# Latent attention: both score halves in a row, then all six transposes, copied in one go

## The chip, the cores and the metric

The kernel runs on one core of a Trainium2 chip. The metric is the device time of one execution in microseconds (us). TensorE does the matmuls and writes to PSUM, which has eight banks of 512 fp32 columns a partition; ScalarE and VectorE read PSUM, GpSimd doesn't; SyncE issues the DMAs.

## The reference

The program is a chain of four blocks over 2,048 tokens of width 128: a state space block, a local transformer of two layers, a latent attention, and a mixture of experts, with a normalisation behind each. The change touches the latent attention alone. Cut to its core, with 16 heads of width 64 and latents of width 64:

```
c_q, c_kv = h @ w_down_q.T, h @ w_down_kv.T
q = rope((c_q @ w_up_q.T) by head)
k = rope((c_kv @ w_up_k.T) by head)
v = (c_kv @ w_up_v.T) by head
attn = softmax(q k.T / 8)
out = (attn v) @ w_out.T + residual
```

Every head attends to all 2,048 keys. All of it is in float32.

## The kernel before, in words

`latent_attention` works through units: a unit is one head and 512 queries (64 units in all), and a step `G` is 128 queries of a unit against the 2,048 keys, so a unit has four steps `r` = 0 to 3. Two heads form a pair with common projections; the loop goes over pairs of heads (four bodies with two pairs each), quarters of the queries `j`, the two heads `w`, and `r`. Eight steps (`w` = 0 and 1, `step` = 4w + r) make one pass; there are 32 passes.

For each step, in two halves of 1,024 keys: TensorE computes the scores into two PSUM banks (`score_pair`, line 1553), VectorE takes the row maximum (`row_max`, 1584), ScalarE the exponential with its sum (`exps`, 1598) into `probs`. Of each half the first three 128-column tiles are transposed by TensorE (`turn_tiles`, 1574) into the bank `turned` and copied by ScalarE to `near` (`copy_tiles`, 1578); the other five are transposed in 32x32 blocks by VectorE (`turn_blocks`, 1684), written to memory by a DMA (1690) and read back reordered into `far` (1695). The values (`mix`, 1614) are multiplied with `near` and `far` one unit later, in eight pairs of matmuls spread over the steps: near pairs at r = 3, far pairs two at r = 0, two at r = 1, one at r = 2 (`MIXED_AT`). `take_mixed` (1622) copies the sum, `output` (1628) multiplies it by the head's output matrix into the two banks `side`, `take_output` (1636) copies these, GpSimd adds them up. Into the same two banks `side` TensorE projects queries and keys of the next pair of heads (`pieces`, 1449); `take_piece` (1569) copies one bank each to `raw`, from which GpSimd makes keys and queries (`make_parts`, 1704, 1455, 1460).

The order of each engine is written out by hand in its block; engines meet at semaphores. The scores of a step are computed one step ahead: in step `G` TensorE issues the scores of `G + 1`, each half as soon as the exponential of that half of `G` has read its banks, and the transposes of `G`. In program order a step of TensorE is: scores of half 0, three transposes, scores of half 1, three transposes, the output products (at step 0 and 6), the values, the pieces (behind the values of step 1 and 3). ScalarE does: what the step has besides (takes, see the listing), copy of half 0, exponential of half 0 of `G + 1`, copy of half 1, exponential of half 1. VectorE does: block transpose of half 1 of `G`, row maxima of both halves of `G + 1`, block transpose of half 0 of `G + 1`. `turned` has one bank, so each group of three transposes waits for the copy of the group before it.

Of the kernel before, what the change touches and what calls it, by code (L numbers as in the profile page):

```python
# [9 lines left out]
ACT = mybir.ActivationFunctionType  # L10
AX = mybir.AxisListType

P = 128
# [3 lines left out]
CH = 512  # L17
# [1285 lines left out]
UNITS = HEADS_G * NC  # L1303
RT = 4
# [3 lines left out]
TURN = NEAR // 2  # L1308
# [5 lines left out]
def latent_attention(nc, dram, const, x, acc):  # L1314

    ident = const["ident"]
# [4 lines left out]
    with Space(nc, "g") as sp:  # L1321
# [4 lines left out]
        with Space(nc, "ga") as s:  # L1326
# [5 lines left out]
            turned = s.ps("turned", [P, 2, CH])  # L1332
# [224 lines left out]
        def pieces(pe, turn, at):  # L1557

            for swap in range(2):
                for kind in range(2):  # L1560
                    ins = projected(side[:, kind, swap * QH:(swap + 1) * QH], turn, kind, swap,
                                    slice(at * QH, (at + 1) * QH))
                    if swap:
                        ins.then_inc(m["piece_full"], 1)

        def take_piece(act, half, kind):
            act.wait_ge(m["parts_ready"], 2 * half + 1 + kind)
            act.wait_ge(m["piece_full"], 2 * half + 1 + kind)
            nc.scalar.activation(raw[:, kind], side[:, kind], ACT.Copy).then_inc(m["piece_taken"], 1)  # L1569

        def turn_tiles(pe, r, half):
            for k in range(TURN):
                at = half * 2 * CH + k * P
                ins = nc.tensor.transpose(turned[:, k * P:(k + 1) * P], probs[:, r % 2, at:at + P], ident[:])  # L1574
            ins.then_inc(m["turn_done"], 1)

        def copy_tiles(act, w, r, half):
            nc.scalar.activation(near[:, w, TURN * half:TURN * (half + 1), r * P:(r + 1) * P],  # L1578
                                 turned[:, 0:TURN * P].rearrange("p (t n) -> p t n", n=P), ACT.Copy).then_inc(m["near_copied"], 1)

# [117 lines left out]
        def make_parts(pool, turn, at, half, kind):  # L1698

            both = raw[:, kind]  # L1700
            first, second = both[:, 0:QH], both[:, QH:]
            n = 8 * half + 3 * kind
            pool.wait_ge(m["piece_taken"], 2 * half + 2 + kind)
            nc.gpsimd.tensor_tensor(both, both, waves[:, at].rearrange("p s n -> p (s n)"), ALU.mult)\  # L1704
                .then_inc(m["order"], 1)
            pool.wait_ge(m["order"], n + 1)
            if kind == 0:
                for head in range(2):
                    place_keys(nc.gpsimd, turn, head, at, QH, first, second).then_inc(m["order"], 1)
                    pool.wait_ge(m["order"], n + 2 + head)  # L1710
            else:
                for crossed in range(2):
                    for head in range(2):
                        place_queries(nc.gpsimd, turn, head, head ^ crossed, at, QH, first, second)\
                            .then_inc(m["order"], 1)
                    pool.wait_ge(m["order"], n + 3 + 2 * crossed)
            pool.sem_inc(m["parts_ready"], 1)
# [3 lines left out]
        with nc.Block() as block:  # L1721

            @block.sync
            def _(sync):
                with sync.Fori(0, PAIRS_G // 2) as i:
                    for turn in range(2):
                        g = 2 * i + turn
                        for j in range(NC):
                            for w in range(2):
# [10 lines left out]
                                if j == 0 and w == 0:  # L1740
                                    sync.wait_ge(m["piece_full"], 2 * H + 2)
                                    load_w(sync, turn, g + 2)
# [41 lines left out]
            def _(pe):  # L1784
# [4 lines left out]
                with pe.Fori(0, PAIRS_G // 2) as i:  # L1789
                    for turn in range(2):  # L1790
                        g = 2 * i + turn
                        for j in range(NC):
                            for w in range(2):
                                U = 8 * g + 2 * j + w
                                for r in range(RT):
                                    G = 4 * U + r
                                    on, head, chunk, at = turn, w, j, r + 1
                                    if r == RT - 1:
                                        head, chunk, at = 1 - w, (j + w) % NC, 0
                                        if w == 1 and j == NC - 1:  # L1800
# [10 lines left out]
                                    if w == 0 and r == 0:  # L1811
                                        pe.wait_ge(m["out_taken"], U + 1)
                                        pe.wait_ge(m["mixed_ready"], U + 1)
                                        pe.wait_ge(mixer_loaded[0], 16 * (4 * g + j + 1))
                                        output(pe, mixer_now[0])
                                    if w == 1 and r == 2:
                                        pe.wait_ge(m["piece_taken"], 2 * (8 * g + 2 * j) + 5)
                                        pe.wait_ge(m["mixed_ready"], U + 1)
                                        pe.wait_ge(mixer_loaded[1], 16 * (4 * g + j + 1))
                                        output(pe, mixer_now[1])  # L1820
                                    if r == 0:
                                        pe.wait_ge(landed[w], 64 * (4 * g + j + 1))
                                    if r == 3:
                                        pe.wait_ge(m["mixed_ready"], U + 2)
                                        pe.wait_ge(m["near_copied"], 8 * U + 1)
                                    mix(pe, w if r < 3 else 1 - w, MIXED_AT[r])
                                    if w == 0 and r == 1:
                                        pe.wait_ge(w_loaded[1 - turn], 16 * (i + 1 + turn))
                                        pe.wait_ge(m["out_taken"], U + 2)
                                        pieces(pe, 1 - turn, 2 * j)  # L1830
                                    if w == 0 and r == 3:
                                        pe.wait_ge(m["piece_taken"], 2 * (8 * g + 2 * j) + 3)
                                        pieces(pe, 1 - turn, 2 * j + 1)
                pe.wait_ge(m["out_taken"], UNITS + 1)
                pe.wait_ge(m["mixed_ready"], UNITS + 1)
                output(pe, mixers[:, HEADS_G + 1])
# [3 lines left out]
                pe.wait_ge(m["near_copied"], 8 * UNITS + 1)  # L1840
                pe.wait_ge(landed[1], 64 * (4 * PAIRS_G + 1))
# [8 lines left out]
            def _(dve):  # L1850
# [30 lines left out]
            def _(act):  # L1881
                act.sem_inc(m["near_copied"], 1)
                act.sem_inc(m["mixed_ready"], 1)
                act.sem_inc(m["piece_taken"], 1)
                act.sem_inc(m["out_taken"], 1)
                for half in range(2):
                    exps(act, 0, 0, half, 0, free=False)
                with act.Fori(0, PAIRS_G // 2) as i:
                    for turn in range(2):
                        g = 2 * i + turn  # L1890
                        for j in range(NC):
                            for w in range(2):
                                U = 8 * g + 2 * j + w
                                H = 8 * g + 2 * j
                                for r in range(RT):
# [5 lines left out]
                                    elif step == 2:  # L1901
                                        take_piece(act, H, 0)
                                        falls(act, H - 1)
                                    elif step == 3:
                                        take_mixed(act, U + 1)
                                        take_piece(act, H, 1)
                                    elif step == 4:
                                        take_piece(act, H + 1, 0)
                                    elif step == 5:
                                        take_piece(act, H + 1, 1)  # L1910
                                    elif step == 6:
# [372 lines left out]
```

## Time and profile before

| | us |
|---|---|
| median of 3 runs (2306.93 to 2310.36) | 2308.57 |
| the profiled execution | 2309.71 |
| its span | 2307.8 |
| TensorE busy (matmuls) | 2063.7 (89%) |
| VectorE busy | 1614.0 (70%) |
| ScalarE busy | 1349.7 (58%) |
| GpSimd busy | 1079.1 (47%) |

The loop of the latent attention runs from about 685 to 2090 us of the span. All times are of one profiled execution. Matmuls are pipelined: a busy TensorE need not be one at its peak, so starts are a better measure than busy times. The clock is that granted to TensorE, as a share of 2.4 GHz.

### The profile page before, as it was taken

To read this page: it belongs to the slowest core of one execution; us is meant where nothing else is said; L and a number is where in the kernel's file an instruction comes from. 1 tells how busy PE (TensorE), PEld (TensorE's weight loads), DVE (VectorE), ACT (ScalarE), POOL (GpSimd) and SP (SyncE) were. 2 spreads that over 40 slices of the span, in tenths; PEclk is the share of its full clock that TensorE was granted. 3 is DMA by queue.
4 is the path that set the end of the run, shared out by engine and by line. 5 is a ranking of instruction groups with operands and counts; after the bars stand their busy time and mean duration, and the time that the engine had idled before them with its cause. 6 is when DMAs were issued, how large, how long until landed. Compare 5 with 4: busy or idle time off the path is not lost. (4 is left out here: it accounts for less than half of the span.)

```text
span 2307.8 us, 37934 instructions
## 1 busy us (share of the span) xinstructions
PE 2063.7 (89%) x11974; PEld 977.9 (42%) x11974; DVE 1614.0 (70%) x2431; ACT 1349.7 (58%) x2907; POOL 1079.1 (47%) x1225
## 2 busy tenths in 40 slices
PE   5848898898669999999999999999999999995597
PEld 2534585476423333333334333333333433432254
DVE  6887665956557777767777776777776777773644
ACT  5425773675117677666776776776766776673111
POOL 0727542833055555545555555555554555553000
PEclk8978899989769999999999999999999999997698
DMA  1001301030145766766766766667666676672000
GB/s 33 1 13 50 72 3 32 1 73 13 52 163 219 255 253 227 261 243 223 259 233 249 260 228 248 225 244 266 227 249 227 238 269 229 245 265 84 35 1 19
DMA packets 195082, 374.26 MB, mean 162 GB/s; under 512 B 11888, under 2 KB 156912, under 8 KB 193840
## 3 DMA queue, kind: packets, MB, share of 16 engines
q1 hardware_dynamic: 194864, 371.61, 45.2%
q8 instruction: 105, 1.72, 0.3%
q14 instruction: 113, 0.93, 0.1%
HBM read 182.82 MB, written 171.44 MB: 154 GB/s over the span
## 5 line engine op out<-in xcount | busy, mean ns | idle before, releaser
L1584 DVE TENSOR_REDUCE g.lowest<-g_score 128x1 f32<-128x1024 f32 x514 | 625.0, 1221 | 217.2 <-PE g_score L1553 214.6
L1598 ACT ACTIVATE g.probs<-g_score,g.lowest 128x1024 f32<-128x1024 f32 x514 | 573.0, 1115 | 117.5 <-DVE g.lowest L1584 117.4
L1553 PE MATMUL g_score<-g.keys,g.queries 64*128 64x512 f32 x2056 | 579.5, 641 | 19.7 <-PEq L1473 10.8
L1684 DVE STREAM_TRANSPOSE g.blocks<-g.probs 128x640 f32<-128x640 f32 x513 | 430.6, 840 | 143.3 <-ACT g.probs L1598 122.8
L1578 ACT ACTIVATE g.near<-g_turned 128x384 f32<-128x384 f32 x512 | 249.7, 488 | 251.0 <-PE g_turned L1574 251.0
L1614 PE MATMUL g_mix_ps<-g.far,mid.y_tok 128*64 128x512 f32 x1320 | 326.0, 607 | 0.0
L1574 PEld LDWEIGHTS g_turned<-top.ident,g.probs 128*128 128x128 f32 x1536 | 159.3, 141 | 391.5 <-issue 198.9
L1574 PE MATMUL g_turned<-top.ident,g.probs 128*128 128x128 f32 x1536 | 281.5, 292 | 0.0
L1553 PEld LDWEIGHTS g_score<-g.keys,g.queries 64*128 64x128 f32 x2056 | 161.9, 186 | 224.5 <-issue 147.9
L1704 POOL TENSOR_TENSOR mid.y_tok<-mid.y_tok,g.waves 128x512 f32<-128x512 f32 x128 | 162.0, 1265 | 192.1 <-ACT mid.y_tok L1569 192.1
L1460 POOL TENSOR_TENSOR g.queries<-mid.y_tok 64x256 f32<-64x256 f32 x256 | 185.2, 724 | 19.6
L1614 PE MATMUL g_mix_ps<-g.near,mid.y_tok 128*64 128x512 f32 x792 | 187.3, 608 | 3.3 <-DMA g.far<-bounce 3.3
L1644 POOL TENSOR_TENSOR g.scaled<-g.scaled,g.coef 128x1024 f32<-128x1024 f32 x67 | 127.1, 1896 | 120.9 <-ACT g.scaled L1636 120.9
L1675 POOL TENSOR_TENSOR g.coef<-g.fall,g.inverse 128x8 f32<-128x8 f32 x65 | 13.2, 202 | 271.9 <-DVE g.inverse L1671 271.9
L1614 PEld LDWEIGHTS g_mix_ps<-g.far,mid.y_tok 128*64 128x64 f32 x1320 | 77.9, 136 | 107.8 <-issue 99.9
L1569 ACT ACTIVATE mid.y_tok<-g_side 128x512 f32<-128x512 f32 x128 | 77.2, 603 | 65.3 <-PE g_side L1449 65.3
L1598 ACT ACTIVATION_READ_ACCUMULATOR g.probs<-g_score,g.lowest 128x1 f32 x514 | 103.1, 201 | 0.0
L1455 POOL TENSOR_TENSOR g.keys<-mid.y_tok 64x256 f32<-64x256 f32 x128 | 92.4, 722 | 10.1
L1614 PEld LDWEIGHTS g_mix_ps<-g.near,mid.y_tok 128*64 128x64 f32 x792 | 51.8, 138 | 93.3 <-issue 93.3
L1650 POOL TENSOR_TENSOR top.x_tok<-top.x_tok,g.scaled 128x512 f32<-128x512 f32 x67 | 85.1, 1270 | 5.3
L1647 POOL TENSOR_TENSOR g.scaled<-g.scaled 128x512 f32<-128x512 f32 x67 | 84.9, 1266 | 5.2
L1636 ACT ACTIVATE g.scaled<-g_side 128x1024 f32<-128x1024 f32 x67 | 69.0, 1030 | 20.6 <-PE g_side L1628 12.6
(364 smaller groups left out, 2893.9 us busy)
## 6 DMA issues: line engine op xcount, KB each, us to landing
g.far<-bounce SPq DMA_DIRECT2D x257, 640.0 KB, 5.8
bounce<-g.blocks SPq DMA_DIRECT2D x256, 640.0 KB, 6.1
g.far<-g.near SPq DMA_DIRECT2D x7, 640.0 KB, 5.7
lt0.v_late<-la0.v SPq DMA_DIRECT2D x6, 512.0 KB, 10.2
lt1.v_late<-la1.v SPq DMA_DIRECT2D x6, 512.0 KB, 10.2
bounce<-g.near SPq DMA_DIRECT2D x4, 640.0 KB, 6.8
top.upto<-g.mixers SPq DMA_DIRECT2D x33, 64.0 KB, 5.6
lt.turns<-turns SPq DMA_DIRECT2D x1, 2048.0 KB, 8.1
```

Of the source, the lines that this page charges most:

```text
L1455: return engine.tensor_tensor(keys[block % 2 * 64:block % 2 * 64 + 64, turn, head, cols], first[head * 64:head * 64 + 64], second[head * 6 ...
L1460: return engine.tensor_tensor(queries[half * 64:half * 64 + 64, turn, head, at * width:(at + 1) * width], first[head * 64:head * 64 + 64], ...
L1553: nc.tensor.matmul(score[:, 2 * pair + odd], queries[rows, turn, head, cols], keys[rows, turn, head, pair * CH:(pair + 1) * CH], start=Tru ...
L1574: ins = nc.tensor.transpose(turned[:, k * P:(k + 1) * P], probs[:, r % 2, at:at + P], ident[:])
L1578: nc.scalar.activation(near[:, w, TURN * half:TURN * (half + 1), r * P:(r + 1) * P], turned[:, 0:TURN * P].rearrange("p (t n) -> p t n", n ...
L1584: nc.vector.tensor_reduce(lowest[:, unit, half, r:r + 1], score[:, 2 * half:2 * half + 2].rearrange("p b n -> p (b n)"), AX.X, ALU.max, ne ...
L1598: nc.scalar.activation(probs[:, r % 2, half * 2 * CH:(half + 1) * 2 * CH], score[:, 2 * half:2 * half + 2].rearrange("p b n -> p (b n)"), ...
L1614: ins = nc.tensor.matmul(out, values[:, at], moving, start=(k == 0), stop=(k == T // 2 - 1))
L1644: nc.gpsimd.tensor_tensor(parts, parts, coef[:, unit].unsqueeze(3).broadcast_to([P, 2, RT, D]), ALU.mult)\
L1650: nc.gpsimd.tensor_tensor(a, a, scaled[:, 0], ALU.add).then_inc(m["added"], 1)
L1684: nc.vector.transpose(blocks[:, r, :, REST * half:REST * (half + 1)].rearrange("p j t c -> p t j c"), probs[:, r % 2, at:at + REST * P].re ...
L1704: nc.gpsimd.tensor_tensor(both, both, waves[:, at].rearrange("p s n -> p (s n)"), ALU.mult)\
```

## The change

Both score halves of a step now stand first, then one wait for the copy of the step before, then all six transposes, into two banks. ScalarE copies the six tiles in one instruction, between its two exponentials. VectorE takes the first row maximum ahead of the block transpose of half 1 of the step before. PSUM has no free bank for this: `turned` and `side` are now three banks with one in common, so in steps 0, 1, 3 and 6 the output products or pieces stand behind the values and wait for the step's own copy, and in steps 1, 2, 4 and 7 the transposes wait until the bank in common has been taken. The pieces of keys and queries are taken by one instruction (steps 2 and 4) in place of two (steps 2 and 3, 4 and 5). The spread of the value pairs over the steps is the same.

```diff
-        turned = sp.ps("turned", [P, CH])
-        side = sp.ps("side", [P, 2, CH])
+        work = sp.ps("work", [P, 3, CH])
+        turned, side = work[:, 0:2], work[:, 1:3]
...
+        def take_pieces(act, half):
+            act.wait_ge(m["parts_ready"], 2 * half + 2)
+            act.wait_ge(m["piece_full"], half + 1)
+            nc.scalar.activation(raw[:], side[:], ACT.Copy).then_inc(m["piece_taken"], 1)
+
+        def turn_tiles(pe, r):
+            for half in range(2):
+                for k in range(TURN):
+                    at = half * 2 * CH + k * P
+                    ins = nc.tensor.transpose(turned[:, half, k * P:(k + 1) * P], probs[:, r % 2, at:at + P], ident[:])
             ins.then_inc(m["turn_done"], 1)
...
+        def copy_tiles(act, w, r):
+            nc.scalar.activation(near[:, w, :, r * P:(r + 1) * P].rearrange("p (k t) n -> p k t n", k=2),
+                                 turned[:, :, 0:TURN * P].rearrange("p k (t n) -> p k t n", n=P), ACT.Copy)\
+                .then_inc(m["near_copied"], 1)
...
-                                    pe.wait_ge(m["exp_done"], 2 * G + 1)
-                                    score_pair(pe, 0, on, head, chunk, at)
-                                    pe.wait_ge(m["near_copied"], 2 * G + 1)
-                                    turn_tiles(pe, r, 0)
-                                    pe.wait_ge(m["exp_done"], 2 * G + 2)
-                                    score_pair(pe, 1, on, head, chunk, at)
-                                    pe.wait_ge(m["near_copied"], 2 * G + 2)
-                                    turn_tiles(pe, r, 1)
...
+                                    for half in range(2):
+                                        pe.wait_ge(m["exp_done"], 2 * G + half + 1)
+                                        score_pair(pe, half, on, head, chunk, at)
+                                    pe.wait_ge(m["near_copied"], G + 1)
+                                    if step == 1:
+                                        pe.wait_ge(m["out_taken"], H + 2)
+                                    elif step == 2:
+                                        pe.wait_ge(m["piece_taken"], H + 1)
+                                    elif step == 4:
+                                        pe.wait_ge(m["piece_taken"], H + 2)
+                                    elif step == 7:
+                                        pe.wait_ge(m["out_taken"], H + 3)
+                                    turn_tiles(pe, r)
...
                                     mix(pe, w if r < 3 else 1 - w, MIXED_AT[r])
+                                    if step in (0, 1, 3, 6):
+                                        pe.wait_ge(m["near_copied"], G + 2)
+                                    if step == 0:
+                                        pe.wait_ge(m["out_taken"], H + 1)
+                                        pe.wait_ge(m["mixed_ready"], U + 1)
+                                        pe.wait_ge(mixer_loaded[0], 16 * (4 * g + j + 1))
+                                        output(pe, mixer_now[0])
...
-                                    turn_blocks(dve, r, 1, G)
                                     if r == 3:
                                         dve.wait_ge(m["combined"], U + 2)
-                                    for half in range(2):
-                                        row_max(dve, unit, (r + 1) % RT, half, G + 1)
+                                    row_max(dve, unit, (r + 1) % RT, 0, G + 1)
+                                    turn_blocks(dve, r, 1, G)
+                                    row_max(dve, unit, (r + 1) % RT, 1, G + 1)
...
-                                    for half in range(2):
-                                        act.wait_ge(m["turn_done"], 2 * G + half + 1)
-                                        copy_tiles(act, w, r, half)
-                                        exps(act, unit, (r + 1) % RT, half, G + 1)
+                                    exps(act, unit, (r + 1) % RT, 0, G + 1)
+                                    act.wait_ge(m["turn_done"], G + 1)
+                                    copy_tiles(act, w, r)
+                                    exps(act, unit, (r + 1) % RT, 1, G + 1)
```

## Rows read from the trace of the kernel before

**Rows 1.** One stretch of the attention stage: length, busy of each engine, granted clock, DMA.

```profile
1100.00:1300.00 200.00, 200.00 (x1030) 78.48 (x1026) 151.57 (x167) 139.65 (x268) 110.92 (x140) 1.00 0.69 250
```

**Rows 2.** What TensorE's matmuls waited for, 700 to 2100 us: total, times, longest.

```profile
PE g_score L1553 <- issue: 8.9, 3, 3.8
PE g_mix_ps L1614 <- DMA g.far<-bounce: 3.3, 1, 3.3
```

**Rows 3.** Timeline of TensorE over one pass: start, duration, instructions.

```profile
1210.51 1.13 PE L1553 MATMUL g_score<-g.keys,g.queries 64*128 64x512 f32 x4
1211.57 0.55 PE L1574 MATMUL g_turned<-top.ident,g.probs 128*128 128x128 f32 x3
1212.04 1.13 PE L1553 MATMUL g_score<-g.keys,g.queries 64*128 64x512 f32 x4
...
1213.58 1.16 PE L1628 MATMUL g_side<-top.upto,g.mixed 64*128 64x128 f32 x16
1214.67 1.94 PE L1614 MATMUL g_mix_ps<-g.far,mid.y_tok 128*64 128x512 f32 x8
1216.54 1.13 PE L1553 MATMUL g_score<-g.keys,g.queries 64*128 64x512 f32 x4
...
1221.48 1.14 PE L1449 MATMUL g_side<-g.c,g.w_up 64*128 64x256 f32 x8
1222.44 1.02 PE L1553 MATMUL g_score<-g.keys,g.queries 64*128 64x512 f32 x4
...
1225.41 1.08 PE L1614 MATMUL g_mix_ps<-g.far,mid.y_tok 128*64 128x512 f32 x4
1226.42 1.13 PE L1553 MATMUL g_score<-g.keys,g.queries 64*128 64x512 f32 x4
...
1251.22 2.79 PE L1614 MATMUL g_mix_ps<-g.near,mid.y_tok 128*64 128x512 f32 x12
1253.95 1.13 PE L1553 MATMUL g_score<-g.keys,g.queries 64*128 64x512 f32 x4
```

**Rows 4.** Timeline of TensorE where the stage begins, and behind the loop's first turn.

```profile
677.53 3.78 PE L1553 MATMUL g_score<-g.keys,g.queries 64*128 64x512 f32 x8 [10.77 <-PEq L1473]
...
1035.21 2.08 PE L1553 MATMUL g_score<-g.keys,g.queries 64*128 64x512 f32 x4 [2.52 <-issue]
```

**Rows 5.** The first of these two as a stretch of TensorE: busy, then granted clock.

```profile
677.50:681.30 3.80, 3.77 (x10) 0.50 0.01 2
```

**Rows 6.** Timeline of the local transformer: eight transposes in a row at full clock.

```profile
423.24 1.09 PE L726 MATMUL lp_turned<-top.ident,lp1.rotated 128*128 128x128 f32 x8
```

**Rows 7.** Timeline of VectorE and ScalarE over the first step of that pass, and later.

```profile
1211.71 1.23 DVE L1584 TENSOR_REDUCE g.lowest<-g_score 128x1 f32<-128x1024 f32 x1 [0.90 <-PE g_score L1553]
...
1213.05 1.11 ACT L1598 ACTIVATE g.probs<-g_score,g.lowest 128x1024 f32<-128x1024 f32 x1 [0.41 <-DVE g.lowest L1584]
...
1213.25 1.23 DVE L1584 TENSOR_REDUCE g.lowest<-g_score 128x1 f32<-128x1024 f32 x1 [0.31 <-PE g_score L1553]
...
1214.15 0.48 ACT L1578 ACTIVATE g.near<-g_turned 128x384 f32<-128x384 f32 x1
1214.39 0.84 DVE L1684 STREAM_TRANSPOSE g.blocks<-g.probs 128x640 f32<-128x640 f32 x1
1214.52 1.12 ACT L1598 ACTIVATE g.probs<-g_score,g.lowest 128x1024 f32<-128x1024 f32 x1
...
1215.61 1.03 ACT L1636 ACTIVATE g.scaled<-g_side 128x1024 f32<-128x1024 f32 x1
1215.76 0.85 DVE L1684 STREAM_TRANSPOSE g.blocks<-g.probs 128x640 f32<-128x640 f32 x1 [0.53 <-ACT g.probs L1598]
...
1223.55 1.23 DVE L1584 TENSOR_REDUCE g.lowest<-g_score 128x1 f32<-128x1024 f32 x1 [0.91 <-PE g_score L1553]
```

**Rows 8.** Timeline behind the loop: a copy, and matmuls that wait for it.

```profile
2110.21 0.59 ACT L1622 ACTIVATE g.mixed<-g_mix_ps 128x512 f32<-128x512 f32 x1
...
2110.85 1.16 PE L1628 MATMUL g_side<-g.mixers,g.mixed 64*128 64x128 f32 x16 [1.61 <-ACT g.mixed L1622]
```

More of the change, by code:

```diff
@@ L1562, in pieces @@
                                     slice(at * QH, (at + 1) * QH))
[L1563 to L1574, printed above, removed]
+            ins.then_inc(m["piece_full"], 1)
+        def take_pieces(act, half):
[7 more added lines that the diff above has]
+                    ins = nc.tensor.transpose(turned[:, half, k * P:(k + 1) * P], probs[:, r % 2, at:at + P], ident[:])
             ins.then_inc(m["turn_done"], 1)
-        def copy_tiles(act, w, r, half):
-            nc.scalar.activation(near[:, w, TURN * half:TURN * (half + 1), r * P:(r + 1) * P],
-                                 turned[:, 0:TURN * P].rearrange("p (t n) -> p t n", n=P), ACT.Copy).then_inc(m["near_copied"], 1)
+        def copy_tiles(act, w, r):
+            nc.scalar.activation(near[:, w, :, r * P:(r + 1) * P].rearrange("p (k t) n -> p k t n", k=2),
+                                 turned[:, :, 0:TURN * P].rearrange("p k (t n) -> p k t n", n=P), ACT.Copy)\
+                .then_inc(m["near_copied"], 1)
         def row_max(dve, unit, r, half, G):
@@ L1702, in make_parts @@
             n = 8 * half + 3 * kind
-            pool.wait_ge(m["piece_taken"], 2 * half + 2 + kind)
+            pool.wait_ge(m["piece_taken"], half + 1)
             nc.gpsimd.tensor_tensor(both, both, waves[:, at].rearrange("p s n -> p (s n)"), ALU.mult)\
@@ L1740, in _ @@
                                 if j == 0 and w == 0:
-                                    sync.wait_ge(m["piece_full"], 2 * H + 2)
+                                    sync.wait_ge(m["piece_full"], H + 1)
                                     load_w(sync, turn, g + 2)
@@ L1809, in _ @@
-                                    pe.wait_ge(m["near_copied"], 2 * G + 2)
-                                    turn_tiles(pe, r, 1)
[L1811 to L1820, printed above, removed]
+                                    step = 4 * w + r
+                                    H = 8 * g + 2 * j
+                                    for half in range(2):
+                                        pe.wait_ge(m["exp_done"], 2 * G + half + 1)
+                                        score_pair(pe, half, on, head, chunk, at)
@@ L1824, in _ @@
                                         pe.wait_ge(m["mixed_ready"], U + 2)
-                                        pe.wait_ge(m["near_copied"], 8 * U + 1)
+                                        pe.wait_ge(m["near_copied"], 4 * U + 1)
                                     mix(pe, w if r < 3 else 1 - w, MIXED_AT[r])
-                                    if w == 0 and r == 1:
+                                    if step in (0, 1, 3, 6):
[5 more added lines that the diff above has]
+                                        output(pe, mixer_now[0])
+                                    elif step == 1:
                                         pe.wait_ge(w_loaded[1 - turn], 16 * (i + 1 + turn))
-                                        pe.wait_ge(m["out_taken"], U + 2)
                                         pieces(pe, 1 - turn, 2 * j)
-                                    if w == 0 and r == 3:
-                                        pe.wait_ge(m["piece_taken"], 2 * (8 * g + 2 * j) + 3)
+                                    elif step == 3:
                                         pieces(pe, 1 - turn, 2 * j + 1)
+                                    elif step == 6:
+                                        pe.wait_ge(m["mixed_ready"], U + 1)
+                                        pe.wait_ge(mixer_loaded[1], 16 * (4 * g + j + 1))
+                                        output(pe, mixer_now[1])
                 pe.wait_ge(m["out_taken"], UNITS + 1)
                 pe.wait_ge(m["mixed_ready"], UNITS + 1)
+                pe.wait_ge(m["near_copied"], 4 * UNITS + 1)
                 output(pe, mixers[:, HEADS_G + 1])
@@ L1839, in _ @@
                 pe.wait_ge(m["mixed_ready"], UNITS + 2)
-                pe.wait_ge(m["near_copied"], 8 * UNITS + 1)
+                pe.wait_ge(m["near_copied"], 4 * UNITS + 1)
                 pe.wait_ge(landed[1], 64 * (4 * PAIRS_G + 1))
@@ L1883, in _ @@
                 act.sem_inc(m["mixed_ready"], 1)
-                act.sem_inc(m["piece_taken"], 1)
                 act.sem_inc(m["out_taken"], 1)
@@ L1901, in _ @@
                                     elif step == 2:
-                                        take_piece(act, H, 0)
+                                        take_pieces(act, H)
                                         falls(act, H - 1)
@@ L1905, in _ @@
                                         take_mixed(act, U + 1)
-                                        take_piece(act, H, 1)
                                     elif step == 4:
-                                        take_piece(act, H + 1, 0)
-                                    elif step == 5:
-                                        take_piece(act, H + 1, 1)
+                                        take_pieces(act, H + 1)
                                     elif step == 6:
```

## The prediction, made before the changed kernel was run

> **What bounds the kernel now.** I read the table of stretches first. In the latent attention stage TensorE is busy for the whole 200 us, at a granted clock of 1.00, beside VectorE 152, ScalarE 140, GpSimd 111 and DMA at 0.69 [rows 1]. The list of TensorE's waits came next: over 1,400 us there are 12 us in which its matmuls stood idle, 8.9 at the loop's turns and one 3.3 us wait for a DMA at the very end [rows 2]. So the stage goes by what TensorE issues, and I lay that out from the timeline. One pass over a pair of units (eight steps) runs from the scores at 1210.51 to the same scores at 1253.95, 43.44 us [rows 3]. A step's scores, transposes, scores, transposes take 3.07 (1210.51 to 1213.58), output products 1.09, two value pairs 1.87, one pair 1.01, three pairs 2.73, the projection pieces 0.96. Scores right behind pieces are 0.1 shorter (busy 1.02 against 1.13). The pass: 8 x 3.07 + 4 x 1.87 + 2 x 1.01 + 2 x 2.73 + 2 x 1.09 + 2 x 0.96 - 2 x 0.1 = 43.42. This agrees with the trace to 0.02, so no wait costs anything in it. There are 32 passes. Every microsecond of TensorE that goes is worth 32, if nothing else is late.
>
> **What TensorE no longer pays.** Scores to transposes take 1.06, transposes to scores 0.47 [rows 3]. Two scores in a row: eight matmul records at a granted clock of 0.50, the 1.2 GHz level, take 3.78; four take 2.08 in the same state (1.13 at full clock), so the second half adds 1.70, which is 0.85 at full clock [rows 3 to 5]. Hence scores, scores, then transposes after 0.85 + 1.06 = 1.91. Three transposes are busy 0.55 [rows 3] and eight in a row 1.09 [rows 6], 0.108 for each further one; six give 0.87, and what follows starts after 0.47 + 3 x 0.108 = 0.80. The front part of a step becomes 2.71 in place of 3.07. The bounds: scores in a row no better than 1.06 apart (nothing gained), six transposes no better than 2 x 0.47 = 0.94. I take 0.85 and 0.80, because both rows show the same instructions in a row. Saved: 0.36 a step, 2.88 a pass, 92 us in all, if nothing is late.
>
> The Trainium skill speaks against the 0.85. "TensorE: Matmul & The Clock Gate", Part 3, The mechanism, says that a weight load passes matmuls in flight only if its row group is another; the second scores load the same two row groups as the first. By it they would be 1.06 apart. The trace at half clock doesn't bear it out; its own result is the fourth case below.
>
> **What is late next.** In the new order a step has this course, counted from its first scores (S0). The first row maximum starts at 1.20 (1210.51 to 1211.71) [rows 3, 7]. The first exponential starts 1.34 behind it, at 2.54, and the next instruction on ScalarE follows 1.10 to 1.11 later [rows 7]. The result of an exponential is there 1.24 after its start (1214.52, the block transpose at 1215.76) [rows 7]: at 3.78. Now the single copy of six tiles stands at 3.65. ScalarE copies 384 elements in 0.48 and 1024 in 1.03 [rows 7]; between them 768 take 0.81, so the copy ends at 4.46, and TensorE goes on 0.05 later (a copy of 0.59 from 2110.21, matmuls at 2110.85) [rows 8]: 4.52. An upper end for it are two old copies, 2 x 0.48 = 0.96; a lower end is 2 x 0.37 = 0.74, the pace at which ScalarE goes from one on to the next instruction (1214.15 to 1214.52). VectorE now does maximum, block transpose of the old second half, maximum. Row maximum to block transpose is 1.14 (1213.25 to 1214.39), and the block transpose (0.84 busy, less the same overlap of 0.08) takes 0.77, so the second maximum starts at 1.20 + 1.14 + 0.77 = 3.11, where before it started at 2.74 (1213.25 less 1210.51). The second exponential: 3.11 + 1.34 = 4.45 against 4.01 before (1214.52), its result at 5.69. ScalarE is free for it at 3.65 + 0.70 (0.81 less the same overlap of 0.11), so it is the maximum that decides, by 0.1.
>
> TensorE wants the second scores of the next step 0.85 after its S0; before it wanted them at 1.53. The chain moves 0.44 later and the demand 0.68 earlier. Step by step (front 2.71, then values, then what else stands there):
> - Step 0: 2.71 + 1.87 = 4.58; the new wait for the copy (4.52) is just covered; output 1.09: 5.67.
> - Step 1: the same wait, covered by 0.06; pieces: 5.54.
> - Step 2: one value pair, 3.72, but the next S0 needs the first exponential at 3.78: 3.78.
> - Step 3: second scores wanted at 0.85, exponential of step 2 there at 5.69 - 3.78 = 1.91: 1.06 idle. 2.71 + 1.06 + 2.73 + 0.96 = 7.46. Its copy wait ahead of the pieces is covered by the three pairs.
> - Step 4: 4.58. Step 5: the exponential comes at 5.69 - 4.58 = 1.11, 0.26 idle: 4.84.
> - Step 6: values end at 3.72, the output must wait for the copy to 4.52, 0.80 idle: 5.61.
> - Step 7: 2.71 + 2.73 = 5.44.
>
> The sum is 42.92. Two steps stand behind pieces, where the scores are 0.1 shorter and the maximum starts after 1.11 in place of 1.20 (1222.44 to 1223.55) [rows 3, 7], so that chain and demand move together: less 0.2, 42.72. Behind the copy wait in steps 0 and 6 stand more waits. On TensorE a second satisfied wait shows no cost [rows 8]; on ScalarE the exponential with its two waits starts 0.11 behind the maximum's end [rows 7], of which 0.05 is the plain signal. I take 0.07 in each of the two steps: 42.86. That is 0.58 less a pass than before (43.44), 18.6 us over 32. Of the 2.88 saved, about 2.3 come back as idle time.
>
> **The other edits.** One take of 1024 in place of two of 512: ScalarE has 30% of the stage free [rows 1]. The take of the pieces (step 2 and 4) and of the outputs (1 and 7) must now precede the transposes, as they share a bank. A take starts about 0.2 after S0, ends 1.03 later [rows 7], at 1.3; transposes come at 1.81 or 1.91. Covered by 0.5. Queued behind such a wait would be transposes, values and the next scores. GpSimd gets both kinds of a half together and must be done with both by step 4 rather than one at a time to step 5; it has 11 us between the two takes, and 45% free [rows 1]; nothing. Blocks written to memory start some 2 us later in their step; the values that need them are issued four steps later, DMA is at 0.69 and TensorE waits for none inside the loop [rows 1, 2]; nothing. The SP queue waits for the joined piece signal once in four passes, far behind it. The turns of the loop (an idle of 2.52 and scores at half clock, once in eight passes and so three times [rows 4]) stay. Value pairs are spread two, two, one, three before as after.
>
> The profiled execution took 2309.7 for a span of 2307.8; the sum against it is 2309.7 - 18.6 = 2291.1. The median of the runs is 1.1 lower, so I forecast 2290.
>
> **Rivals.**
> 1. The waits are covered after all: the full 92 us come, 2217. For it: each wait hangs on latencies of tenths, and only four of the eight steps show one. Against: step 3 lacks 1.06 and step 6 0.80, more than any error in a row. Half of the waits gone would give 2255.
> 2. Slower: the order S0, first exponential, copy, second exponential is later than I lay it out. One delay d of exponentials and copy hits steps 3, 5 and 6 in full, step 0 in full (its margin is used up by the 0.07) and step 1 beyond 0.06; some 5d - 0.06 a pass. It decides from d = 0.13 (0.58 gone). The copy at its upper end (two old copies) is 0.15 later for the output and 0.06 for the exponential, about 0.5 a pass, 16 us: no change, 2306. At d = 0.25 it is 1.19 - 0.58 = 0.6 a pass: 2328. For it: the copy reads two separate stretches and ScalarE and VectorE take turns with no slack left. Against: all parts have rows.
> 3. Transposes gain nothing by being six (0.94): steps 0, 1, 4, 7 and 3 lose 0.14, step 5's wait stays as it hangs on step 4: 0.6 or 0.7 a pass, 2309 to 2312, no change. Against: [rows 6].
> 4. The switch between the two scores is not hidden (1.06, as by the page above). Worked out as above: steps 0, 1, 4, 7 +0.21 each, step 2 +0.15, step 3 -0.15, step 5 -0.05, step 6 nothing; +0.8 a pass, 0.2 over before, 2315. Against: [rows 4, 5].
>
> **Chances.** The forecast (2278 to 2302) 0.58; gain beyond it 0.14; rival 2 0.18, a third of it within 0.2%; rival 3 0.05; rival 4 0.05. A measurement of this kernel tells 0.2% (4.6 us) from no change. Faster 0.73, within 0.2% 0.13, slower 0.14. The range takes in half of the gain beyond and rival 2's copy bound: 2266 to 2312.
>
> **What would show it.** Right: a pass of about 42.9 between equal scores; scores to scores some 0.85 to 0.96 and six transposes busy 0.87; TensorE idle about 1.06 ahead of the second scores of step 3, released by the exponential, and about 0.8 ahead of the output of step 6, released by the copy; TensorE busy for less than the full stretch; second exponential 4.45 after S0. Wrong: no idle there (rival 1), idle ahead of the outputs and pieces in steps 0 and 1 too (rival 2), a copy over 0.9, or score starts 1.06 apart (rival 4), a fallen clock in the stage, or waits for landed blocks inside the loop.

## The result, and the profile after

The changed kernel takes 2268.26 us (median of 4 runs, 2266.51 to 2268.74) against 2309.47 for the kernel before (2306.93 to 2311.29): a ratio of 0.9821, 95% interval 0.9804 to 0.9838. That is 41 us less. The forecast was the right way and in the range, but of the wrong size: 18.6 us less, under half of what came. The measured time lies 2 us inside the lower end of the range (2266), and outside the narrower 2278 to 2302 that was given a chance of 0.58.

The first view is the same stretch as in [rows 1]: TensorE is no longer busy throughout, at the same clock of 1.00, VectorE and ScalarE are about as busy as before.

```profile
1100.00:1300.00 200.00, 193.03 (x1066) 83.26 (x1064) 148.82 (x173) 140.06 (x232) 113.39 (x141) 1.00 0.72 248
```

The second is what TensorE's matmuls waited for from 700 to 2100 us (total, times, longest). Beside the loop's turns and the one wait for a DMA, which were the whole of [rows 2], two new waits stand here, 32 times each or nearly so: once a pass. (Waits of the blocks behind the attention are left out.) They are the output of step 6 that waits for the copy, and the second scores of step 3 that wait for the exponential.

```profile
PE g_work L1629 <- ACT g.near L1578: 24.5, 34, 1.2
PE g_score L1553 <- ACT g.probs L1599: 21.4, 32, 0.7
...
PE g_score L1553 <- issue: 8.5, 3, 3.1
PE g_mix_ps L1615 <- DMA g.far<-bounce: 2.8, 1, 2.8
```

The third is the timeline of TensorE over a pass, to be laid beside [rows 3] (start, duration, instructions). It begins with the scores of step 1.

```profile
1202.60 1.89 PE L1553 MATMUL g_score<-g.keys,g.queries 64*128 64x512 f32 x8
1204.42 0.87 PE L1574 MATMUL g_work<-top.ident,g.probs 128*128 128x128 f32 x6
1205.22 1.94 PE L1615 MATMUL g_mix_ps<-g.far,mid.y_tok 128*64 128x512 f32 x8
1207.09 1.14 PE L1449 MATMUL g_work<-g.c,g.w_up 64*128 64x256 f32 x8
1208.06 1.88 PE L1553 MATMUL g_score<-g.keys,g.queries 64*128 64x512 f32 x8
...
1210.67 1.08 PE L1615 MATMUL g_mix_ps<-g.far,mid.y_tok 128*64 128x512 f32 x4
1211.76 1.13 PE L1553 MATMUL g_score<-g.keys,g.queries 64*128 64x512 f32 x4
1213.55 1.13 PE L1553 MATMUL g_score<-g.keys,g.queries 64*128 64x512 f32 x4 [0.67 <-ACT g.probs L1599]
...
1219.11 1.88 PE L1553 MATMUL g_score<-g.keys,g.queries 64*128 64x512 f32 x8
...
1223.60 2.14 PE L1553 MATMUL g_score<-g.keys,g.queries 64*128 64x512 f32 x8
1225.67 0.88 PE L1574 MATMUL g_work<-top.ident,g.probs 128*128 128x128 f32 x6
...
1228.34 1.99 PE L1553 MATMUL g_score<-g.keys,g.queries 64*128 64x512 f32 x8
1230.26 0.88 PE L1574 MATMUL g_work<-top.ident,g.probs 128*128 128x128 f32 x6
1231.06 1.08 PE L1615 MATMUL g_mix_ps<-g.far,mid.y_tok 128*64 128x512 f32 x4
1232.84 1.16 PE L1629 MATMUL g_work<-top.after,g.mixed 64*128 64x128 f32 x16 [0.70 <-ACT g.near L1578]
1233.84 1.89 PE L1553 MATMUL g_score<-g.keys,g.queries 64*128 64x512 f32 x8
...
1239.18 1.99 PE L1553 MATMUL g_score<-g.keys,g.queries 64*128 64x512 f32 x8
...
1243.77 1.16 PE L1629 MATMUL g_work<-top.upto,g.mixed 64*128 64x128 f32 x16
1244.77 1.89 PE L1553 MATMUL g_score<-g.keys,g.queries 64*128 64x512 f32 x8
```

From scores to the same scores it is 42.17 (1202.60 to 1244.77) where it was 43.44: 1.27 less, and 32 passes make 40.6 of the 41 us. The reader is to see two things. Scores to transposes to values take 1.92 + 0.80 (1228.34, 1230.26, 1231.06), as laid out (1.91 + 0.80). The idle time that the profile prints (0.67, 0.70) is smaller than what is lost, since a matmul's printed duration goes on beyond the time at which the next could start: four score matmuls print 1.13 where the next could start after 0.85, a value pair 1.08 where the next work started after 1.01. By starts, step 3 loses 1.79 - 0.85 = 0.94 and step 6 loses 1.78 - 1.01 = 0.77.

The fourth is ScalarE and VectorE in step 6, for [rows 7].

```profile
1229.54 1.23 DVE L1585 TENSOR_REDUCE g.lowest<-g_score 128x1 f32<-128x1024 f32 x1 [0.91 <-PE g_score L1553]
...
1230.88 1.11 ACT L1599 ACTIVATE g.probs<-g_score,g.lowest 128x1024 f32<-128x1024 f32 x1 [1.64 <-DVE g.lowest L1585]
...
1231.44 1.19 DVE L1585 TENSOR_REDUCE g.lowest<-g_score 128x1 f32<-128x1024 f32 x1
...
1231.99 0.80 ACT L1578 ACTIVATE g.near<-g_work 128x768 f32<-128x768 f32 x1
...
1232.68 1.11 ACT L1599 ACTIVATE g.probs<-g_score,g.lowest 128x1024 f32<-128x1024 f32 x1
```

The copy takes 0.80 and ends at 1232.79; the output starts at 1232.84 (third view). The first exponential starts 1.34 behind its maximum, the second 1.24 behind its own and 0.69 behind the start of the copy (1231.99 to 1232.68).

### The profile page after: what moved, and what is told of

Same layout as the page of the kernel before. It is cut to its first block and busy times, and to the rows that moved or that the text cites. A ratio compares the mean times of both kernels' runs of the same rounds, so it can differ in the third digit from the quotient of the medians.

```text
span 2266.1 us, 37473 instructions
## 1 busy us (share of the span) xinstructions
PE 1976.2 (87%) x11974; PEld 991.2 (44%) x11974; DVE 1559.9 (69%) x2431; ACT 1313.2 (58%) x2587; POOL 1078.8 (48%) x1225
## 5 line engine op out<-in xcount | busy, mean ns | idle before, releaser
L1585 DVE TENSOR_REDUCE g.lowest<-g_score 128x1 f32<-128x1024 f32 x514 | 618.2, 1203 | 371.2 <-PE g_score L1553 371.2
L1553 PE MATMUL g_score<-g.keys,g.queries 64*128 64x512 f32 x2056 | 513.9, 612 | 40.8 <-ACT g.probs L1599 21.4
L1685 DVE STREAM_TRANSPOSE g.blocks<-g.probs 128x640 f32<-128x640 f32 x513 | 425.8, 830 | 0.9
L1553 PEld LDWEIGHTS g_score<-g.keys,g.queries 64*128 64x128 f32 x2056 | 175.6, 187 | 294.7 <-issue 148.4
L1574 PEld LDWEIGHTS g_work<-top.ident,g.probs 128*128 128x128 f32 x1536 | 163.8, 141 | 194.8 <-issue 146.3
L1574 PE MATMUL g_work<-top.ident,g.probs 128*128 128x128 f32 x1536 | 224.6, 282 | 0.0
L1578 ACT ACTIVATE g.near<-g_work 128x768 f32<-128x768 f32 x256 | 205.3, 802 | 0.6 <-PE g_work L1574 0.6
L1568 ACT ACTIVATE mid.y_tok<-g_work 128x1024 f32<-128x1024 f32 x64 | 65.6, 1025 | 70.9 <-PE g_work L1449 70.9
L1637 ACT ACTIVATE g.scaled<-g_work 128x1024 f32<-128x1024 f32 x67 | 68.7, 1025 | 34.0 <-PE g_work L1629 25.9
```

What stands on the lines that cost most here:

```text
L1553: nc.tensor.matmul(score[:, 2 * pair + odd], queries[rows, turn, head, cols], keys[rows, turn, head, pair * CH:(pair + 1) * CH], start=Tru ...
L1574: ins = nc.tensor.transpose(turned[:, half, k * P:(k + 1) * P], probs[:, r % 2, at:at + P], ident[:])
L1578: nc.scalar.activation(near[:, w, :, r * P:(r + 1) * P].rearrange("p (k t) n -> p k t n", k=2), turned[:, :, 0:TURN * P].rearrange("p k (t ...
L1585: nc.vector.tensor_reduce(lowest[:, unit, half, r:r + 1], score[:, 2 * half:2 * half + 2].rearrange("p b n -> p (b n)"), AX.X, ALU.max, ne ...
L1685: nc.vector.transpose(blocks[:, r, :, REST * half:REST * (half + 1)].rearrange("p j t c -> p t j c"), probs[:, r % 2, at:at + REST * P].re ...
```

## Experiments

Each was timed in rounds with the kernel before on the same chip; the ratio is to that kernel. Beside it I give the pass, read from the starts of the output products, as [rows 3] give it for the kernel before (43.44); it is free of what differs outside the loop.

**1. The output products behind the values, in the kernel before.**

```diff
-                                    if w == 0 and r == 0:
-                                        ...
-                                        output(pe, mixer_now[0])
...
                                     mix(pe, w if r < 3 else 1 - w, MIXED_AT[r])
+                                    if w == 0 and r == 0:
+                                        ...
+                                        output(pe, mixer_now[0])
```

(and the same for step 6)

> The kernel before, with one edit: the output products of step 0 and 6 stand behind the values instead of ahead of them. Theory (the switch of TensorE's work was mis-sized): output to scores takes 1.00 in place of output to values 1.09, and the scores behind the output are 0.10 shorter, so 0.19 for each of the two outputs of a pass, 0.38 x 32 = 12 us faster than the kernel before (ratio 0.995), a pass of 43.06 in place of 43.44. Rival: these tenths come only with two score halves in a row; then nothing, within 2 us of before.

Measured: ratio 0.9942 (0.9929 to 0.9954), 15 us less by the medians, 13 by the ratio and 12 by the passes; the pass is 43.06, as the theory said. TensorE's timeline in step 0 and 1:

```profile
1209.60 1.94 PE L1614 MATMUL g_mix_ps<-g.far,mid.y_tok 128*64 128x512 f32 x8
1211.47 1.16 PE L1628 MATMUL g_side<-top.upto,g.mixed 64*128 64x128 f32 x16
1212.46 1.03 PE L1553 MATMUL g_score<-g.keys,g.queries 64*128 64x512 f32 x4
1213.42 0.55 PE L1574 MATMUL g_turned<-top.ident,g.probs 128*128 128x128 f32 x3
```

The output takes 0.99 to the scores in place of 1.09 to the values [rows 3], and the scores behind it 0.96 to the transposes in place of 1.06. So 12 us of the changed kernel's gain have nothing to do with scores in a row: they come from the new place of the output, which the prediction had booked at nothing.

**2. VectorE's new order alone, in the kernel before.**

```diff
-                                    turn_blocks(dve, r, 1, G)
...
-                                    for half in range(2):
-                                        row_max(dve, unit, (r + 1) % RT, half, G + 1)
+                                    row_max(dve, unit, (r + 1) % RT, 0, G + 1)
+                                    turn_blocks(dve, r, 1, G)
+                                    row_max(dve, unit, (r + 1) % RT, 1, G + 1)
```

> The kernel before, with VectorE's new order alone (first row maximum, block transpose of the old second half, second row maximum). Theory: it moves the second exponential some 0.35 later in a kernel where TensorE wants it late; a wait of at most 0.1 in step 3, so 0 to 4 us slower than before. Rival: the new order itself is part of the gain (VectorE waits less for the exponential); then faster than before by over 5 us.

Measured: 1.0053 (1.0038 to 1.0068), 12 us more by the ratio and 8 by the passes (43.70). The sign is that of the theory and the rival falls; the size is larger than the 0 to 4 us it gave. A wait stands in the trace once a pass, of a kind that it had not counted, for the old single bank of transposes:

```profile
PE g_turned L1574 <- ACT g.near L1578: 6.3, 32, 0.2
```

This run also shows how soon an exponential can follow its maximum when ScalarE has nothing else to do: the second one starts 1.22 behind, with ScalarE idle for 0.20 ahead of it.

```profile
1221.13 1.19 DVE L1584 TENSOR_REDUCE g.lowest<-g_score 128x1 f32<-128x1024 f32 x1
1222.35 1.12 ACT L1598 ACTIVATE g.probs<-g_score,g.lowest 128x1024 f32<-128x1024 f32 x1 [0.20 <-DVE g.lowest L1584]
```

**3. VectorE's old order, in the changed kernel** (the diff of 2 the other way round).

> The changed kernel with VectorE's old order (block transpose of the old second half, then both row maxima). Theory: the block transpose waits for the second exponential and stands ahead of the first row maximum, so the first exponential and the copy come later where a step is short; the output of step 6 waits 1.2 in place of 0.8 and the second scores behind step 5 half a microsecond: some 0.9 a pass, 29 us slower than the changed kernel, 12 us faster than the kernel before (ratio 0.995). Rival (VectorE's order is of no matter, TensorE's own work sets the time): as the changed kernel, ratio 0.982.

Measured: 0.9919 (0.9897 to 0.9941), a little under the 0.995 of the theory; a pass of 43.05, 0.88 more than the changed kernel's, its 0.9. The rival falls. What TensorE's matmuls waited for:

```profile
PE g_work L1629 <- ACT g.near L1578: 34.0, 32, 1.1
PE g_score L1553 <- ACT g.probs L1599: 29.1, 64, 0.7
```

The wait of the output in step 6 has grown and a second wait for the exponential has come (in step 6, ahead of the second scores). The order that costs 8 to 12 us in experiment 2 is worth 23 us here (2291.68 less 2268.26, from two chips; 28 us by the passes): the same edit has the opposite sign once the exponentials' chain is what TensorE waits for.

**4. The copy later: two small ScalarE copies ahead of it,** in the changed kernel. They compute nothing that is used.

```diff
+                                    nc.scalar.activation(const["ones"][:], ident[:], ACT.Copy)
+                                    nc.scalar.activation(const["ident16"][:], ident[:], ACT.Copy)
                                     copy_tiles(act, w, r)
```

> The changed kernel with two small ScalarE copies of 128 columns ahead of the copy of six tiles in each step; they compute nothing that is used. Theory (the chain first exponential, copy, second exponential sets where TensorE waits): copy and second exponential come some 0.3 later; the full delay hits steps 3, 5 and 6, most of it steps 0 and 1: about 1.3 a pass, 40 us slower than the changed kernel, ratio to before 0.998 to 1.002. Rival (the waits have slack, ScalarE has 30% free): under 10 us slower than the changed kernel, ratio below 0.987.

Measured: 1.0055 (1.0041 to 1.007), above the 0.998 to 1.002 of the theory; a pass of 44.03, 1.86 more than the changed kernel's (the theory had 1.3), 60 us over 32 passes and 54 by the ratios. ScalarE and TensorE around the output of step 6:

```profile
1208.57 1.19 DVE L1585 TENSOR_REDUCE g.lowest<-g_score 128x1 f32<-128x1024 f32 x1
...
1209.11 0.30 ACT L1926 ACTIVATE top.ones<-top.ident 128x128 f32<-128x128 f32 x1
1209.31 0.30 ACT L1927 ACTIVATE top.ident<-top.ident 128x128 bf16<-128x128 f32 x1
1209.51 0.80 ACT L1578 ACTIVATE g.near<-g_work 128x768 f32<-128x768 f32 x1
...
1210.20 1.11 ACT L1599 ACTIVATE g.probs<-g_score,g.lowest 128x1024 f32<-128x1024 f32 x1
...
1210.36 1.16 PE L1629 MATMUL g_work<-top.after,g.mixed 64*128 64x128 f32 x16 [1.09 <-ACT g.near L1578]
```

The copies delay the tiles' copy by 0.40 (1209.11 to 1209.51), not by 0.3; the prediction's second rival put a delay d at 5d - 0.06 a pass, which is 1.94. By starts, the waits of steps 3, 5 and 6 have grown by 0.40, 0.39 and 0.39, and new ones of 0.38 and 0.30 stand ahead of the output of step 0 and the pieces of step 1: 1.86. So 0.4 us a step (3.2 a pass) on an engine that is 30% free cost 1.86 a pass. The rival with slack falls. By the same slope a delay of 0.27 a step would eat the whole gain of 1.27 (an estimate from this one run). The second exponential follows the copy's start by 0.69 again (1209.51 to 1210.20), though its maximum has ended 0.44 before.

**5. The value pairs spread two, two, two, two,** in the changed kernel. The third near pair moves to the next r = 0, where the copy waits for it.

```diff
-        MIXED_AT = (range(3, 5), range(5, 7), range(7, 8), range(0, 3))
+        MIXED_AT = (range(2, 4), range(4, 6), range(6, 8), range(0, 2))
...
+                if k == TURN - 1:
+                    ins.then_inc(m["near_read"], 1)
...
-            elif pairs[0] == 0:
-                ins.then_inc(m["near_read"], 1)
...
-                                    if r == 0:
-                                        act.wait_ge(m["near_read"], U + 1)
...
                                     exps(act, unit, (r + 1) % RT, 0, G + 1)
+                                    if r == 0:
+                                        act.wait_ge(m["near_read"], U + 1)
                                     act.wait_ge(m["turn_done"], G + 1)
```

> The changed kernel with the value pairs spread two, two, two, two over the steps r = 0 to 3; the third near pair moves from r = 3 to the r = 0 behind it, and the copy of that step waits for it. Theory (the idle time sits where a step has one value pair only): the 0.94 ahead of the second scores of step 3 and the 0.77 ahead of the output of step 6 go, some 0.2 waits come in steps 1, 3 and 5; a pass of about 40.8 to 41.0 in place of 42.17, 38 to 43 us faster than the changed kernel, ratio to before 0.963 to 0.966. Rival (each wait moves on to the next step, as the exponentials' chain bounds the mean and not single steps): within 10 us of the changed kernel, 0.978 to 0.982.

Measured: 0.9681 (0.966 to 0.9701), 32 us less than the changed kernel by the ratios, where the theory had 38 to 43 (0.963 to 0.966) and the rival under 10; a pass of 41.09, a little over the 40.8 to 41.0. The rival falls: most of the idle time belongs to the steps with one pair and does not move on. A part does. TensorE around steps 3, 5 and 0:

```profile
1160.93 2.14 PE L1553 MATMUL g_score<-g.keys,g.queries 64*128 64x512 f32 x8
1163.00 0.87 PE L1574 MATMUL g_work<-top.ident,g.probs 128*128 128x128 f32 x6
...
1171.13 2.35 PE L1553 MATMUL g_score<-g.keys,g.queries 64*128 64x512 f32 x8
1173.40 0.88 PE L1574 MATMUL g_work<-top.ident,g.probs 128*128 128x128 f32 x6
...
1231.21 1.03 PE L1615 MATMUL g_mix_ps<-g.far,mid.y_tok 128*64 128x512 f32 x4
1232.37 1.16 PE L1629 MATMUL g_work<-top.upto,g.mixed 64*128 64x128 f32 x16
```

Scores to transposes in step 3 are 2.07, so 0.16 idle where it was 0.94. In step 5 they are 2.27, so 0.36 idle where it was 0.16, and in step 0 2.06 to 2.07, 0.15 where there was none. The output of step 0 starts 1.16 behind the last value pair, where scores start 0.96 behind it: 0.20 of wait, as its copy waits for the near pair. Neither of these two in step 0 was among the waits that the theory named (steps 1, 3 and 5).

**6. The copy last in steps 2, 4, 5 and 7,** in the changed kernel: there nothing waits for the step's own copy.

```diff
                                     exps(act, unit, (r + 1) % RT, 0, G + 1)
+                                    if (step in (2, 4, 5, 7)):
+                                        exps(act, unit, (r + 1) % RT, 1, G + 1)
                                     act.wait_ge(m["turn_done"], G + 1)
                                     copy_tiles(act, w, r)
-                                    exps(act, unit, (r + 1) % RT, 1, G + 1)
+                                    if not (step in (2, 4, 5, 7)):
+                                        exps(act, unit, (r + 1) % RT, 1, G + 1)
```

(and on VectorE in these steps both row maxima, then the block transpose)

> The changed kernel; in steps 2, 4, 5 and 7, where nothing waits for the step's own copy, ScalarE does both exponentials and then the copy, and VectorE both row maxima and then the block transpose. Theory (the second exponential behind the copy makes the idle time ahead of the second scores): it comes 0.7 earlier in these steps, the wait of step 3 falls from 0.94 to 0.25, that of step 5 goes; the wait of 0.77 ahead of the output of step 6 stays: a pass of 41.3, 28 us faster than the changed kernel, ratio 0.970. Rival (the late copy or VectorE's late block transpose delays transposes or exponentials of the next step): no faster than the changed kernel.

Measured: 0.9697 (0.9677 to 0.9716), a pass of 41.31, the 41.3 of the theory. The waits for the exponential are gone from the list, those for the copy stay (22.4 us, 33 times, against 24.5 and 34), which is what tells the two apart. By starts 0.25 of idle time is left in step 3, as the theory said: scores to transposes take 2.16 there.

```profile
1198.92 2.23 PE L1553 MATMUL g_score<-g.keys,g.queries 64*128 64x512 f32 x8
1201.08 0.88 PE L1574 MATMUL g_work<-top.ident,g.probs 128*128 128x128 f32 x6
```

**7. Both of these.**

> Both edits on the changed kernel: the even spread, and the copy last in steps 2, 4, 5 and 7. Theory: nearly all idle time of TensorE in the loop is gone; a pass of 40.2, which is the sum of TensorE's own pieces (8 x 2.71 + 8 x 1.87 + 2 x 1.00 + 2 x 0.97 - 4 x 0.10 = 40.2), 62 us faster than the changed kernel, ratio 0.955. Rival: another engine's chain (VectorE 74% busy, DMA at 0.72) takes over before; then over 41 a pass.

Measured: 0.9595 (0.9567 to 0.9623), 2218.14 us, where the theory had 0.955, and a pass of 40.45 in place of 40.2. The rival (over 41) falls. This is the best of the kernels. TensorE's stretch, its step 0, and ScalarE's copy in that step:

```profile
1100.00:1300.00 200.00, 199.14 (x1109) 88.22 (x1107) 153.15 (x178) 145.13 (x238) 118.17 (x149) 1.00 0.75 263
```

```profile
1219.90 1.08 PE L1615 MATMUL g_mix_ps<-g.near,mid.y_tok 128*64 128x512 f32 x4
1220.81 1.03 PE L1615 MATMUL g_mix_ps<-g.far,mid.y_tok 128*64 128x512 f32 x4
1221.97 1.16 PE L1629 MATMUL g_work<-top.upto,g.mixed 64*128 64x128 f32 x16
```

```profile
1221.02 0.81 ACT L1578 ACTIVATE g.near<-g_work 128x768 f32<-128x768 f32 x1
```

TensorE is busy throughout again. No other engine has taken over. Of the 0.25 over the sum of the pieces, 0.20 is the wait of the output of step 0 (1220.81 to 1221.97, 1.16 in place of 0.96): the copy starts only at 1221.02, when the near pair is through (1219.90 + 1.08), and the output 0.14 behind the copy's end. Against the passes (2.99 x 32 = 96 us less than before) the ratio gives 94, and 0.955 would have been 104; the loop's three turns cost more here: 16.85, 17.07 and 17.61 from output to output where 10.29 is usual, 20.7 over it together, against 15.10, 16.22 and 16.43 where 10.97 is usual in the kernel before (14.8 over it) and 14.74, 14.95 and 15.69 and 10.93 in the changed kernel (12.6). Why, no run tells.

## Why the prediction was right or wrong

**What bounds the kernel:** right. All of the gain is in what TensorE issues and waits for in the pass (40.6 of 41 us).

**What TensorE no longer pays:** right. Scores in a row take 1.91 to the transposes, six transposes 0.80 to what follows, busy 0.87. The forecast's 2.71 a step is what a step without idle time shows. The fourth rival would have 2.1 from scores to transposes; the trace has 1.91 with the same row groups twice, so it falls. The rule of the Trainium skill ("TensorE: Matmul & The Clock Gate", Part 3, The mechanism) that only another row group lets a weight load pass would give that 2.1, so here the measurement differs from the rule. The same section of the Trainium skill also lets a load go ahead when it targets the background weight buffer, which the prediction did not weigh; with this the 1.91 agrees. The third rival (0.94 for six) falls too.

**What is late next:** the places are right, the sizes were not all. The idle time in step 3 (0.94, forecast 1.06), step 6 (0.77, forecast 0.80 + 0.07) and step 5 (0.16, forecast 0.26) is there, in steps 3 and 6 released by what was named (step 5's is too short to stand in the list of waits), and steps 0 and 1 have none. Experiments 3 to 6 move each by the edit that should move it. Step by step, from S0 to S0, in order of steps 0 to 7: forecast, with the credit behind pieces and the two 0.07, 5.74, 5.54, 3.68, 7.46, 4.48, 4.84, 5.68, 5.44, sum 42.86; measured 5.59, 5.46, 3.70, 7.35, 4.49, 4.74, 5.50, 5.34, sum 42.17. So 0.69 a pass, 22 us, are missing from the forecast. The steps of the prediction that failed are these terms, each small and all of one sign:

- The output products. The sum kept 1.09 for each, a duration read where they stood ahead of the values, and gave the scores behind them the full length. In the new place they take 1.00, and the scores behind them are 0.1 shorter, as behind pieces. Steps 0, 1, 6 and 7: 0.37 a pass, 12 us. Experiment 1 shows it by itself. The prediction moved the output with its old figure and did not ask what then stands behind it, though it gave the same credit for the scores behind pieces.
- The second exponential. The prediction put it 1.34 behind its maximum, at 4.45, and had ScalarE free for it at 4.35, "so it is the maximum that decides, by 0.1". It starts at 4.34 (1228.34 to 1232.68): ScalarE's own pace decides. In 255 of the 256 steps it starts 0.69 behind the start of the copy, and it does so too where its maximum has ended long before, by 0.44 in experiment 4 and by 0.78 in experiment 3. The 1.34 is what is seen behind the first maximum; behind a second one 1.22 is enough (experiment 2), so the two bounds lie within some 0.02 here and the copy's is the later. That is 0.11 in step 3 and 0.10 in step 5, 7 us.
- The stacked waits. Two allowances of 0.07 were added for satisfied waits behind the copy's. In step 6 the output starts 0.05 behind the copy's end with its two further waits, in step 0 it starts on time behind the values, 0.14 after the copy has ended: neither costs anything, 0.14 a pass, 4.5 us. Where the copy does come last in step 0, it is 0.13 to 0.14 from its end to the output (experiments 4 and 7). The trace tells the two steps apart: in step 0 an instruction of TensorE's sequencer (line 1830, the wait for the output matrix) stands between the copy's end and the output in every pass, in step 6 there is none. So the allowance was not wrong as such, but not due here.

Together 0.72 against 0.69. None of them is one of the rivals: the first rival (the waits covered) would have had no idle time, and it is there.

**The other edits:** nothing for the merged takes, DMA and GpSimd, right as far as the list of waits shows: TensorE waits for none of them inside the loop, and every pass but the three with the loop's turns agrees to 0.2. No run takes these edits back one by one. VectorE's order was part of the chain as laid out; that the changed kernel needs it is shown by experiment 3.

## What to carry to other kernels

The cost of a piece of work on TensorE depends on what stands ahead of it and behind it: when a piece is moved, take the start-to-start times of the new neighbours, or bound the switch, and don't carry its old figure along. When a change takes work from the busy engine, lay out the chain that fed it in starts, step by step: the new waits come out in the right steps and right to about a tenth even where the total does not, and the steps with the least cover (here those with one value pair) name the next edit. Ask of each link whether it waits for its input or for its engine: the second exponential was put down to its maximum, and it was ScalarE's copy ahead of it. An engine that is 30% free can be the bound: 0.4 us a step on ScalarE's chain cost 1.86 us a pass of eight steps.

## What was not expected of the hardware

- One half of scores behind other 64-row work (output products or pieces) takes 0.96 to the transposes, behind the 128-row values or transposes 1.06, in the kernel before and in experiment 1; two halves take 1.82 and 1.92 in the changed kernel.
- From the end of a row maximum to the start of the exponential it is 0.11 behind the first maximum (1230.77 to 1230.88), with ScalarE idle, but 0.03 to 0.04 behind the second in experiment 2 (1222.32 to 1222.35), with ScalarE idle as well. Why the two differ, no run tells.
- Once in four passes, where the next pair of heads is taken up, a pass is 0.19 longer in the changed kernel (11.12 in place of 10.93 from output to output); it is not there in the kernel before. In these passes three instructions of TensorE's sequencer (lines 1828 to 1830, the output's further waits) stand between the copy's end and the output of step 0 in place of one, and the output starts 0.33 behind the copy's end in place of 0.14.
